# A decoder layer on one core: the recurrence's front two iterations earlier, and the expert result rows found on GpSimd

## The reference

```
x = layernorm(x + (x + mamba(x)))           # the recurrence
x = layernorm(x + cross_attention(x, ctx))  # 16 heads, rotary positions
x = layernorm(x + experts(x))               # shared expert + top 3 of 15 experts
```

## Time and profile before

| | us |
|---|---|
| median of 3 runs | 2185.69 (2179.36 to 2189.15) |
| profiled execution | 2181.16 |
| its span | 2179.3 |
| recurrence, first to last scan | 66 to 953 |
| expert tiles, first to last store | 1677.7 to 2042.3 |

### The profile page before, as it was taken

How to read it: one execution, slowest core, us unless ns; L and a number is a source line. 1 busy time by engine, 2 the same in 40 slices (tenths; PEclk the granted TensorE clock), 3 DMA queues, 4 the chain that set the end, 5 groups by cost and what they waited for, 6 DMA issues and landing times. The chain is left out here.

```text
span 2179.3 us, 32460 instructions
## 1 busy us (share of the span) xinstructions
PE 1697.8 (78%) x9684; PEld 1089.3 (50%) x9685; DVE 1588.5 (73%) x2792; ACT 1042.0 (48%) x2354; POOL 1248.0 (57%) x840
## 2 busy tenths in 40 slices
PE   5688778778777778534787888777498999999695
PEld 4344444444444444213455555555385555555484
DVE  3699999999899999965478888875223555555278
ACT  3677777777777777620233333333112333333221
POOL 0889888898889899847547776633200222222100
PEclk9899998999899999657799999988699999999897
DMA  5544444555554455414833333331541222222332
GB/s 162 116 115 114 113 111 108 116 117 117 117 117 116 103 123 114 111 60 97 211 106 109 123 105 113 110 106 38 177 163 36 79 82 82 80 81 82 139 128 77
DMA packets 178820, 238.24 MB, mean 109 GB/s; under 512 B 24001, under 2 KB 114113, under 8 KB 176642
## 3 DMA queue, kind: packets, MB, share of 16 engines
q1 hardware_dynamic: 161426, 201.73, 35.4%
q0 software_dynamic: 9984, 28.06, 3.6%
q10 hardware_dynamic: 7280, 6.83, 1.2%
HBM read 169.70 MB, written 66.84 MB: 109 GB/s over the span
## 5 line engine op out<-in xcount | busy, mean ns | idle before, releaser
L268 POOL TENSOR_TENSOR inject<-dx_n,bc_n 128x2048 f32<-128x2048 f32 x128 | 578.9, 4533 | 147.5 <-DMA dx_n<-dup_rows 84.7
L401 ACT ACTIVATE ps_h<-delta_n,a_neg 128x256 f32<-128x256 f32 x1024 | 424.9, 462 | 110.9 <-DVE hc L537 73.5
L524 DVE TENSOR_TENSOR_SCAN ps_h<-ps_h,inject 128x1024 f32<-128x1024 f32 x160 | 365.9, 2287 | 23.8 <-ACT ps_h L401 23.8
L1951 POOL DMA_INDIRECT token_results<-e_y,e_y_row x112 | 106.9, 955 | 389.8 <-DVE e_y L2013 389.5
L1114 ACT ACTIVATE expT<-ps_t 128x512 f32<-128x512 f32 x256 | 147.6, 593 | 307.9 <-PE ps_t L1496 305.7
L1192 DVE TENSOR_REDUCE neg_max<-ps_s 128x2 f32<-128x512 f32 x256 | 172.2, 676 | 123.4 <-PE ps_s L1485 122.9
L524 DVE TENSOR_TENSOR_SCAN h_pool<-ps_h,inject 128x1024 f32<-128x1024 f32 x96 | 218.6, 2278 | 18.9 <-POOL inject L268 14.5
L277 POOL TENSOR_TENSOR h_pool<-h_pool,bc_n 128x1024 f32<-128x1024 f32 x96 | 225.7, 2351 | 0.0
L2041 PE MATMUL e_ps_h<-w,e_xT 128*128 x448 | 219.5, 613 | 7.7 <-issue 6.6
L537 DVE TENSOR_TENSOR hc<-ps_h,bc_n 128x1024 f32<-128x1024 f32 x160 | 195.7, 1223 | 5.9
L1485 PE MATMUL ps_s<-Ks,Qs 96*128 96x256 bf16 x512 | 103.8, 286 | 45.4 <-DVE neg_max L1192 34.9
(11 more groups left out here) (274 smaller groups left out, 3453.0 us busy)
## 6 DMA issues: line engine op xcount, KB each, us to landing
delta_n<-dup_rows SPq DMA_DIRECT2D x128, 256.0 KB, 4.6
dx_n<-dup_rows SPq DMA_DIRECT2D x128, 256.0 KB, 7.6
bc_n<-bc_rows SPq DMA_DIRECT2D x64, 256.0 KB, 4.5
xg<-slot_rows SPq DMA_DIRECT2D x112, 136.0 KB, 2.1
Ks<-k_rows SPq DMA_DIRECT2D x192, 64.0 KB
Qs<-q_rows SPq DMA_DIRECT2D x192, 64.0 KB
e_rows_in<-token_results SPq DMA_DIRECT2D x8, 1536.0 KB, 18.9
dup_rows<-delta SPq DMA_DIRECT2D x32, 256.0 KB, 6.4
```

Of the source, the lines that this page charges most:

```text
L268: nc.gpsimd.tensor_tensor(inject[:, at:at + 2, :, :], dx_n[c // 2][:, None, :, c % 2, :].to_broadcast([P, 2, JB, L]), bc_n[b % 2][:, 0, nq ...
L401: last = nc.scalar.activation(ps_h[k % 2][:, j, :], delta_n[c // 2][:, j, c % 2, :], ACT.Exp, scale=a_neg[:, c, nq, j:j + 1])
L524: nc.vector.tensor_tensor_scan(out.rearrange("p j t -> p (j t)"), ps_h[k % 2][:, :, :].rearrange("p j t -> p (j t)"), inject[:, k % RING, ...
L1951: g.indirect_dma_start(out=y_dram, out_offset=bass.IndirectOffsetOnAxis(ap=y_row[:, j:j + 1], axis=0), in_=y[j][:, 0, :], in_offset=None). ...
```

## The change

In the recurrence, all of the front is put earlier: convolutions of b + 2 at i = 13 to 15 of b, silus at i = 0, take_db at 2, the exponentials at 3 and 5, the logarithms at 4 and 6, delta at 6 and 8 (the first ahead of the second logarithm), dx at 7 and 9, norm_x at 7, scale_xT at 9, projections from 9 on. skip gets a third buffer. xn has no tile of its own any more but lies in zln. The residual is added in X itself, and res goes. In the experts, spare tiles are 14 instead of 16 (110 in all). Padding rows bring their own row in the dump with them (fill, spare_rows, made on the host and loaded), so that the result row needs no arithmetic; GpSimd copies it (find_rows) two tiles ahead of the store. VectorE's order in a step becomes take_h, take_y, multiply.

```diff
-SLOT_TILES = (T * TOPK // P + NE + 1) // 2 * 2
+SLOT_TILES = T * TOPK // P + NE - 1
-        xn = sb("xn", [P, TT, D])
+        xn = zln[:, 0:2, :]
-        skip = [sb(f"skip{j}", [P, EC, L]) for j in range(2)]
+        skip = [sb(f"skip{j}", [P, EC, L]) for j in range(SKIPS)]
             def norm_x(b):
                 if b >= 1:
                     act.wait_ge(f_tr, b)
+                    act.wait_ge(f_sp, (b - 2) * 2 + 3 if b >= 2 else 1)
             # silus
                 if b >= 2:
-                    act.wait_ge(gated, (b - 1) * EC)
+                    act.wait_ge(s_sum, hc_count((b - 2) * ITERS + ITERS - 3))
-                nc.scalar.activation(skip[q][:, :, :], skip_raw[:, :, :], ACT.Silu).then_inc(f_u, 1)
+                if b >= SKIPS:
+                    act.wait_ge(gated, (b - SKIPS + 1) * EC)
+                nc.scalar.activation(skip[b % SKIPS][:, :, :], skip_raw[:, :, :], ACT.Silu).then_inc(f_u, 1)
             # ScalarE, before the loop: norm_x(1) behind take_delta(0, 1)
             # ScalarE, in the loop
                 make_decay(k + 2)
+                if front and i == 0:
+                    silus(b + 1)
                 if front and i == 2:
-                    silus(b + 1)
+                    take_db(b + 1)
+                if front and i in (3, 5):
+                    softplus_exp(b + 1, (i - 3) // 2)
                 if front and i == 4:
-                    take_db(b + 1)
-                if front and i in (5, 7):
-                    softplus_exp(b + 1, (i - 5) // 2)
-                if front and i in (6, 8):
-                    softplus_log(b + 1, (i - 6) // 2)
+                    softplus_log(b + 1, 0)
+                if front and i == 6:
+                    take_delta(b + 1, 0)
+                    softplus_log(b + 1, 1)
                 if tail and i == 7:
                     layernorm_root(b - 1)
-                if front and i in (8, 10):
-                    take_delta(b + 1, (i - 8) // 2)
+                if front and i == 8:
+                    take_delta(b + 1, 1)
+                if entry and i == 7:
+                    norm_x(b + 2)
                 if entry and i == 9:
-                    norm_x(b + 2)
-                if entry and i == 11:
                     scale_xT(b + 2)
+                if entry and i in (10, 11):
+                    take_xin(b + 2, i - 10)
                 if entry and i in (12, 13):
-                    take_xin(b + 2, i - 12)
-                if entry and i in (14, 15):
-                    take_skip(b + 2, i - 14)
-                if tail and i == 13:
+                    take_skip(b + 2, i - 12)
+                if tail and i == 14:
                     normalize(b - 1)
             # VectorE
-                if b < B - 1 and i in (9, 11):
-                    make_dx(b + 1, (i - 9) // 2)
+                if b < B - 1 and i in (7, 9):
+                    make_dx(b + 1, (i - 7) // 2)
             # TensorE, in the loop
                 sums(b, i)
-                if front and i in (0, 1):
-                    conv(b + 1, i + 1)
-                if front and i == 1:
-                    conv(b + 1, 3)
+                if front and i == 2:
+                    project_db(b + 1)
                 if tail and i == 3:
                     project_out(b - 1)
-                if front and i == 4:
-                    project_db(b + 1)
-                if front and i == 5:
+                if front and i == 3:
                     half_z(b + 1, 0)
                     half_z(b + 1, 1)
-                if front and i in (7, 9):
-                    add_softplus(b + 1, (i - 7) // 2)
-                if entry and i == 10:
+                if front and i in (5, 7):
+                    add_softplus(b + 1, (i - 5) // 2)
+                if entry and i == 8:
                     transposes(b + 2)
+                if entry and i in (9, 10):
+                    project_in(b + 2, i - 9)
                 if entry and i in (11, 12):
-                    project_in(b + 2, i - 11)
-                if entry and i in (13, 14):
-                    project_skip(b + 2, i - 13)
+                    project_skip(b + 2, i - 11)
+                if entry and i >= 13:
+                    conv(b + 2, i - 13)
                 if entry and i == 15:
-                    conv(b + 2, 0)
+                    conv(b + 2, 3)
             # attention, SP
-                    sp.dma_start(zero_v[:, NE * REGION:NE * REGION + spare, :],
-                                 ffn.zero[:, :].unsqueeze(1).to_broadcast([P, spare, XW])).then_inc(zeroed, 16)
+                    sp.dma_start(slots_dram[NE * REGION * P:, :], dram["spare_rows"]).then_inc(zeroed, 16)
             # expert tiles, SP
                     sp.wait_ge(e_hid, t + AHEAD + 1)
+                    sp.wait_ge(e_rows, t + AHEAD + 1)
             # expert tiles, GpSimd
+            def find_rows(t):
+                at = t % ROWS
+                e = expert(g, t)
+                g.wait_ge(x_in[t % R], 16 * (t // R + 1))
+                if t >= ROWS:
+                    g.wait_ge(y_out[t % R], 16 * ((t - ROWS) // R + 1))
+                nc.gpsimd.tensor_copy(y_row[:, at:at + 1], xg[t % R][:, bass.ds(e + D, 1)]).then_inc(e_rows, 1)
+            for t in range(AHEAD):
+                find_rows(t)
+            for t in range(SLOT_TILES):
+                if t + AHEAD < SLOT_TILES:
+                    find_rows(t + AHEAD)
+                send(t)
             # expert tiles, VectorE
-                nc.vector.tensor_copy(code[:, j % R:j % R + 1], xg[j % R][:, bass.ds(e + D, 1)])
-                nc.vector.tensor_tensor(y_row[:, j:j + 1], code[:, j:j + 1], lane[:, bass.ds(t, 1)], ALU.max)
                 if left > 2:
                     take_h(t + 2, j + 2)
+                take_y(i, j)
+                if left > 2:
                     multiply(t + 2, j + 2)
-                take_y(i, j)
```

More of the change, by code:

```diff
@@ L416, in _ @@
             silus(0)
-            norm_x(1)
             take_db(0)
@@ L423, in _ @@
             take_delta(0, 1)
+            norm_x(1)
             root(REST, 1)
@@ L547, in gate @@
                     v.wait_ge(out_done, b)
-                nc.vector.tensor_tensor(y_gated[:, c, :], ps_y[c % 2][:, 0, :], skip[b % 2][:, c, :],
+                nc.vector.tensor_tensor(y_gated[:, c, :], ps_y[c % 2][:, 0, :], skip[b % SKIPS][:, c, :],
                                         ALU.mult).then_inc(gated, 1)
@@ L560, in row_stats @@
                 for s in range(TT):
-                    last = nc.vector.bn_stats(stats[:, s, :], res[:, s, :])
+                    last = nc.vector.bn_stats(stats[:, s, :], X[:, b * TT + s, 0:D])
                 last.then_inc(row_step, 1)
@@ L759, in _ @@
                 project_skip(1, hf)
-            conv(1, 0)
+            for n in range(EC):
+                conv(1, n)
             for k in range(B * ITERS):
@@ L1175, in set_pads @@
             def set_pads():
-                nc.vector.memset(ffn.zero[:, :], 0.0).then_inc(zero_made, 1)
                 for q in range(2):
@@ L1872, in _, with expert_phase @@
                     last.then_inc(turned, 1)
-def expert_phase(nc, ident, ffn, w1, b1, b2, lane, expert_of, tile_of, slots_dram, y_dram):
+def expert_phase(nc, ident, ffn, w1, b1, b2, expert_of, tile_of, slots_dram, y_dram):
     with ExitStack() as ctx:
@@ L1903, in expert_phase @@
         y_out = [sem(f"e_y_out{j}") for j in range(R)]
+        e_rows = sem("e_rows")
         e_tr, e_xT, e_h, e_hid, e_gate, e_act, e_ta, e_aT, e_yp, e_y = (
@@ L1916, in steps @@
                     body(i, j, 2 * R)
-            for i in (ROUNDS - 2, ROUNDS - 1):
-                for j in range(R):
-                    body(i, j, SLOT_TILES - i * R - j)
+            for t in range((ROUNDS - 2) * R, SLOT_TILES):
+                body(t // R, t % R, SLOT_TILES - t)
         def expert(eng, t):
@@ L1935, in _ @@
                     sp.wait_ge(e_hid, t - R + 1)
+                    sp.wait_ge(e_rows, t - R + 1)
                 load_x(t, t)
@@ L1947, in _, with send @@
         def _(g):
-            for t in range(SLOT_TILES):
+            def find_rows(t):
[5 more added lines that the diff above has]
+                nc.gpsimd.tensor_copy(y_row[:, at:at + 1], xg[t % R][:, bass.ds(e + D, 1)]).then_inc(e_rows, 1)
+            def send(t):
                 j = t % R
+                g.wait_ge(e_rows, t + 1)
                 g.wait_ge(e_y, t + 3)
                 g.indirect_dma_start(
-                    out=y_dram, out_offset=bass.IndirectOffsetOnAxis(ap=y_row[:, j:j + 1], axis=0),
+                    out=y_dram, out_offset=bass.IndirectOffsetOnAxis(ap=y_row[:, t % ROWS:t % ROWS + 1], axis=0),
                     in_=y[j][:, 0, :], in_offset=None).then_inc(y_out[j], 16)
+            for t in range(AHEAD):
[4 more added lines that the diff above has]
+                send(t)
             for j in range(R):
-                g.wait_ge(y_out[j], 16 * ROUNDS)
```

(8 more changed lines are left out.)

43 lines of the change are left out of this document (21 added, 22 removed).

## The result

| | before | after |
|---|---|---|
| median (same chip, 4 runs each) | 2182.53 us (2177.78 to 2189.15) | 2158.18 us (2156.34 to 2160.09) |
| ratio | | 0.9894, 95% interval 0.9873 to 0.9916 |
| profiled execution, span | 2181.16, 2179.3 | 2160.09, 2158.3 |

What follows compares the result with a forecast made beforehand. It took VectorE to bound the recurrence and TensorE the expert tiles. 2181.2 - 0.8 (start) - 0.4 + 12.9 + 0.1 (recurrence) - 0.3 (attention) - 6.6 (tiles) = 2186.1 us, range 2165 to 2205.

Steps and rivals of the forecast that it cites:

- TensorE sets this pace: Expert tiles: TensorE full, so VectorE's slack buys nothing; cost 0 (-8 to +3), beside -6.6 us for two fewer tiles.
- Rival 3: Expert tiles speed up to 3.21 us each, 8 us off, total 2179; chance 10%.
- Silu batch at i = 0: Recurrence: VectorE waits 2.60 us before scan 3 instead of 1.30 before scan 5, +1.30 us per sequence.
- The dx wait goes: Recurrence: delta's first half is ready before make_dx at i = 7, so 1.18 us per sequence go.
- The new wait before scan 12: Recurrence: scan 12 waits for sums(10) behind a half-clock project_in, 0.6 to 0.9 us, taken as +0.80 per sequence.
- rival 4: Recurrence: half clock holds through sums(10), scan 12 waits 2.5 us and more; 22 us more, total 2208; chance 17%.
- rival 1: Recurrence: no new wait before scan 12, project_in at full clock or ScalarE ahead; 10.4 us go, total 2175.7; chance 24%.
- The sum of the recurrence: From the first scan to the recurrence's last gate, forecast 12.6 us longer, at +0.99 for each of 13 sequences.
- The first sequence: Sequence 0 of the recurrence: loses ScalarE waits, gets a longer one before scan 3; -0.4 us (-2 to +2).
- The start: Before the first scan: norm_x(1) leaves the place ahead of take_db(0) on ScalarE, -0.8 us (0 to -0.9).
- GpSimd's dx_n wait: Recurrence: GpSimd's 5.7 us gap per sequence is slack and falls under 2 us after the change.
- The +0.07 of delta's second half: Recurrence: delta's second half is ready 5.8 us after scan 8's start, just when hc 9 is done; +0.07 us per sequence.

Runs made afterwards that it cites:

- e5: Kernel before with VectorE's order take_h, take_y, multiply and TensorE's expert number for down loaded ahead of turn_a: 2150.24 against 2183.02 us, ratio 0.9834.
- e2: Kernel before with TensorE's expert number for down loaded ahead of turn_a, not behind it: 2184.27 against 2182.40 us, ratio 1.0003.
- e9: Changed kernel with the old front, take_delta ahead of the logarithm at i = 8, down's expert number loaded ahead of turn_a: 2116.01 against 2185.10 us.
- e6: Changed kernel with projections, take_xin and take_skip of b + 2 one iteration later, so sums(10) precedes project_in: 2148.06 against 2183.02 us, ratio 0.9844.
- e10: Kernel of e9 with the silu batch at i = 3 instead of i = 2: 2109.77 against 2185.10 us, ratio 0.9674.
- e7: Kernel before with delta's first half ahead of the second logarithm at i = 8 on ScalarE: 2167.39 against 2183.02 us, ratio 0.9925.
- e1: Kernel before with only VectorE's order in an expert step changed to take_h, take_y, multiply: 2177.05 against 2182.40 us, ratio 0.9965.

## Why the prediction was wrong

The profiled time is 26.0 us under the forecast (2186.1 - 2160.1). 15.1 of them are in the expert tiles, 6.6 in the start and the recurrence, 3.3 in attention, 0.9 in the rest.

**The step that failed: "TensorE sets this pace: it is busy 97.7 of 100 us there" ... "it gets slack, which buys nothing while TensorE is full".** Its bound of the gain, TensorE's idle 2.3%, was taken from the same number. The term was 0 and measured -15.1 (109 x 0.139). Two things were wrong in it. TensorE was not full: with both limits lifted it does the same work in 2.998 instead of 3.285 us (e5), 9% less. And VectorE had no slack: its round of 3.27 us had no wait for TensorE in it and was as long as the pitch of three tiles in four (e2, e9). Rival 3 named the mechanism, "VectorE's chain of register loads and the gelu no longer runs close behind TensorE", but gave it 3.21 us a tile, 8 us and 10%, because the same 97.7 stood against it. The row that decided was in the trace: VectorE's timeline of three tiles in four, whose idle times are all "issue" or its own gelu. The prediction quoted one of its lines and used it only for the price of a GpSimd copy.

The Trainium skill ("Perfetto Trace Analysis", Identifying the Most-Contended Engine) says that matmul busy time does not tell how close TensorE is to its limit, and to look at the useful arithmetic and the weight loads' share instead. This trace agrees: matmuls 97.7% and weight loads 57.1% before, 100.0% and 61.6% when the pace was really TensorE's (e5), so the second number grew by 8%, nearly as much as the pace, and the first by 2%. The same section finds the bottleneck engine by occupancy and calls it a fair measure for VectorE; here it was 54% and VectorE was a limit (e2), and the measurement decides.

**The recurrence, step by step.**
- Silu batch at i = 0: a wait of 2.60 us before scan 3 forecast, 2.53 measured (scan 3's decay is ready 525.81 - 514.98 = 10.83 us after scan 0's start, forecast 10.82), and none before scan 5. Right. e6, which keeps it, and e10, which moves it the other way and gets 1.02, bear it out.
- The dx wait goes: right. The forecast had put it down to the order of delta and the logarithm, and e7 shows that this order alone is the cause.
- The new wait before scan 12: its place and its releaser right (e6 takes it away). project_in starts 8.36 us behind scan 8's start, forecast 8.3. Forecast 0.6 to 0.9 us in 13 sequences, 10.4 in sum; measured 14.7 in sum over 12 waits (two of them put down to ScalarE), from 0.5 to 2.4 us. The size of one was off, since the clock came back at different times: late in some sequences, as rival 4 said, in time in others, and in two sequences project_in had the full clock from its start and there was no wait, as rival 1 said. That the sum came near is the mean of these three cases, and so in part luck. In TensorE's timeline after the change, one sequence and the next:

```profile
548.79 0.66 PE L638 MATMUL ps_a<-ident,zln 128*128 128x128 f32 x4
552.53 3.78 PE L646 MATMUL ps_b<-xnT,w_in 128*128 128x256 f32 x8 [3.07 <-ACT xnT L319]
556.24 1.08 PE L702 MATMUL ps_y<-u,d_diag 128*32 128x256 f32 x8
557.09 1.08 PE L716 MATMUL ps_y<-hc,sel 128*32 128x256 f32 x8
557.95 0.89 PE L716 MATMUL ps_y<-h_pool,sel 128*32 128x256 f32 x8
...
609.81 3.62 PE L646 MATMUL ps_b<-xnT,w_in 128*128 128x256 f32 x8 [4.00 <-ACT xnT L319]
613.36 0.64 PE L702 MATMUL ps_y<-u,d_diag 128*32 128x256 f32 x8
613.82 0.61 PE L716 MATMUL ps_y<-hc,sel 128*32 128x256 f32 x8
614.25 0.61 PE L716 MATMUL ps_y<-h_pool,sel 128*32 128x256 f32 x8
```

And one of the two at full clock (granted 1.00 from 440.72 to 442.64):

```profile
440.72 1.99 PE L646 MATMUL ps_b<-xnT,w_in 128*128 128x256 f32 x8 [3.49 <-ACT xnT L319]
```

- The sum of the recurrence: +12.6 forecast from the first scan on, +7.0 measured. What the forecast left out is that the kernel before was not regular: it counted every sequence at 55.24 us, while some took 56.1 to 59.0, scan 5 to scan 5. After the change they took 55.2 to 57.3. Over 15 periods that is 7.5 us above the regular ones before and 15.2 after, so against a regular kernel before, the cost would have been somewhat over the forecast and not half of it. The long ones before have longer waits for ScalarE's decays, at scan 5 and three times at scan 2 (4.0 us, the longest 2.9); what makes ScalarE late there was not tried, and it differs from one execution to the next. The first sequence was forecast 0.4 shorter and was 1.3 longer.
- The start: -0.8 forecast, -1.8 measured. In all traces the first scan begins at 66.1 to 68.3 with the old start and at 64.2 to 65.4 with the new one, so the gain is real and perhaps larger than either.
- GpSimd's dx_n wait was to fall under 2 us in each sequence: right, 7.5 us are left over 11 waits, the longest 1.5. The gap was slack, as forecast: before the change VectorE waited for an inject at the start and hardly after it (0.5 us), so there was nothing to earn.
- Three small readings are off: the end of hc 9 stands once as 5.82 and once as 5.87, and the 1.18 us before dx are a mean with long waits in it; in regular sequences it is 1.13. The +0.07 of delta's second half has no row behind it, and after the first sequence no wait before dx is in the trace.

**The sum.** The recurrence's large terms came out with the right sign and nearly the right size, the wait before scan 12 as a mean of unlike cases; the whole was forecast at no change and came out 1.1% faster because the term that was held at zero was the largest.

## What to carry to other kernels

Before a stage is called bound by an engine at 98%, follow one round of every engine that meets it: a round that has no wait for the others and is as long as the pitch is a limit too, however idle its engine looks. Edits tried one at a time then find nothing (e2) or little (e1) where both together give 32 us (e5). Read the pitch tile by tile, too: a mean can hide one late tile in each turn of the loop. Issue register loads ahead of a wait, not behind it, where another engine sets off that wait (e9; alone, e2 gained nothing). Put a batch that holds up a producer where its consumer has most work in hand, not where its own data is ready first (2.53 us of wait at i = 0, 1.30 at i = 2, 1.02 at i = 3).

## What the runs showed of the hardware

- A register load ahead of an instruction cost VectorE 0.45 to 0.51 us of "issue" for an operation of 0.15 us. On TensorE it took some 0.9 us from the end of the product that it waited for to down's first weight load, when the load of the register stood behind that wait. Neither counts as busy, and the matmul behind it is recorded as longer: down's first took 0.478 us when late and 0.38 when not.
- TensorE's clock did not come back after a fixed piece of work. project_in started behind 3.1 us of idle time at one sequence and 4.0 at the next and took 3.78 and 3.62 us, at a granted clock of 0.50 and 0.53, so at 1.2 GHz for all or nearly all of it; the three groups of sums behind it took 1.08, 1.08 and 0.89 us in the one and 0.64, 0.61 and 0.61 in the other, the time at 2.4 GHz. In a third sequence it started behind 3.5 us of idle time and took 1.99 us at a granted clock of 1.00.
- The turn of the loop on TensorE's queue (0.21 us of branch) made up's first matmul 0.37 to 0.43 us late in that tile where a register load stood behind turn_a's wait (0.48 and 0.55 us instead of 0.11 and 0.12), and not at all where that load stood ahead of it and the product came early (e5, e9).
- GpSimd's store took 0.976 us instead of 0.954 when the copy of the row code stood on GpSimd too; nobody waited for it.
